# One core: recurrence and experts in halves of 512 rows, experts in whole fp32

## What is computed

```python
# recurrence, x after a layer norm; q, k rotated
q_r = einsum('bthd,hrd->bthr', q, Wq); k_r = einsum('bthd,hrd->bthr', k, Wk)
g = sigmoid(x @ g_w.T + g_b)
def step(M, inp):
    M = M * decay + einsum('bhr,bhd->bhrd', g_t * k_t * scale, v_t)
    y = einsum('bhr,bhrd->bhd', q_t, M)
hres = x + (Y @ out_w.T + out_b); result = layernorm(hres) * ln_g + ln_b
# experts, xt after a layer norm
scores = softmax(xt @ gate_w.T); top two: weights, idx
xs = xt * weight
for e in range(8):
    h = silu(xs @ w1[e].T + b1[e]); x2 = h @ w2[e].T + b2[e]; x3 = xs @ w3[e].T + b3[e]
    y += sum over the two choices of x2 * x3 * (idx == e)
z = silu(xt @ sw1.T) * (xt @ sw2.T) @ sw3.T
result = y + z
```

## Time and profile before

| | us |
|---|---|
| median of three runs | 2244.3 (2242.52 to 2247.84) |
| profiled execution | 2242.04, span 2240.0 |
| granted clock of TensorE, mean of the span | 0.978 |
| PE busy | 2057.9 (92%) |
| DVE busy | 1506.3 (67%) |
| ACT busy | 1309.4 (58%) |
| POOL busy | 1429.1 (64%) |

### The profile page before, as it was taken

How to read it: one execution, slowest core, us unless ns; L and a number is a source line. 1 busy time by engine, 2 the same in 40 slices (tenths; PEclk the granted TensorE clock), 3 DMA queues, 4 the chain that set the end, 5 groups by cost and what they waited for, 6 DMA issues and landing times. The chain is left out here.

```text
span 2240.0 us, 47860 instructions
## 1 busy us (share of the span) xinstructions
PE 2057.9 (92%) x19834; PEld 1531.2 (68%) x19834; DVE 1506.3 (67%) x1760; ACT 1309.4 (58%) x1585; POOL 1429.1 (64%) x652
## 2 busy tenths in 40 slices
PE   4799999999999999999999989999999777667998
PEld 3577777767777776777777767777777433215777
DVE  5666666766666667666666676666666247995685
ACT  2477767676767666677777676767676540002332
POOL 0277777777777777777777767777777622552464
PEclk8899999999999999999999999999999889997999
DMA  8010101111010112010001030101000030000320
GB/s 233 15 35 14 27 14 41 44 43 25 15 28 13 28 30 71 13 30 16 25 16 43 16 76 7 34 6 34 13 18 4 4 126 0 0 0 10 119 99 38
DMA packets 44669, 79.77 MB, mean 36 GB/s; under 512 B 7072, under 2 KB 31264, under 8 KB 43696
## 3 DMA queue, kind: packets, MB, share of 16 engines
q1 hardware_dynamic: 44464, 76.80, 12.2%
HBM read 70.03 MB, written 5.31 MB: 34 GB/s over the span
## 5 line engine op out<-in xcount | busy, mean ns | idle before, releaser
L764 POOL TENSOR_TENSOR acc<-acc,PR 128x1024 f32<-128x1024 f32 x480 | 1154.2, 2405 | 348.7 <-ACT PR L545 311.4
L620 DVE TENSOR_REDUCE amx<-ps 128x2 f32<-128x1024 f32 x512 | 626.9, 1224 | 387.4 <-PE ps L318 387.4
L545 ACT ACTIVATE PR<-ps 128x1024 f32<-128x1024 f32 x512 | 518.7, 1019 | 236.3 <-PE ps L326 236.3
L505 ACT ACTIVATE ps<-NM 128x1024 f32<-128x1024 f32 x416 | 427.2, 1028 | 189.3 <-DVE V L605 144.9
L334 PE MATMUL ps<-PR,V 128*64 128x256 f32 x4096 | 504.6, 389 | 0.1
L334 PEld LDWEIGHTS ps<-PR,V 128*64 128x64 f32 x4096 | 273.6, 138 | 163.3 <-issue 33.3
L326 PE MATMUL ps<-qh,KH 64*128 64x256 f32 x2048 | 329.2, 310 | 33.3 <-ACT ps L505 29.6
L300 PE MATMUL ps<-wv,C 64*128 64x256 f32 x4608 | 314.7, 280 | 0.0
L289 PE MATMUL ps<-C,wk 64*128 64x512 f32 x2304 | 311.2, 398 | 0.7 <-DVE x L654 0.7
L300 PEld LDWEIGHTS ps<-wv,C 64*128 64x128 f32 x4608 | 305.3, 186 | 8.4
L326 PE MATMUL ps<-ql,KH 64*128 64x256 f32 x2048 | 300.6, 280 | 0.0
(11 more groups left out here) (168 smaller groups left out, 1847.1 us busy)
## 6 DMA issues: line engine op xcount, KB each, us to landing
wk<-wk_split SPq DMA_DIRECT2D x62, 192.0 KB, 3.2
wv<-wv_split SPq DMA_DIRECT2D x30, 384.0 KB, 5.2
bc<-wm_rows SPq DMA_DIRECT2D x16, 512.0 KB, 5.0
craw<-in_ctx SPq DMA_DIRECT2D x30, 256.0 KB, 3.8
we<-in_we SPq DMA_DIRECT2D x8, 768.0 KB, 6.9
wo<-in_wo SPq DMA_DIRECT2D x68, 64.0 KB, 2.2
wq<-in_wq SPq DMA_DIRECT2D x32, 128.0 KB, 3.0
craw<-in_ctx SPq DMA_DIRECT2D x30, 128.0 KB, 4.0
```

Source lines behind the costliest of these rows:

```text
L505: act.activation(ps[:, first_bank:first_bank + 2, :].rearrange("p h (k n) -> p h k n", k=2), row.unsqueeze(2).to_broadcast([P, 2, 2, ROWS] ...
L545: act.activation(PR[:, pr_slot(t, hf), :, :, :].rearrange("p h k n -> p (h k n)"), ps[:, bank:bank + 2, :].rearrange("p h n -> p (h n)"), ...
L620: dve.tensor_reduce(amx[:, :, t, c], psG, AX.X, ALU.max).then_inc(g_max, 1)
L764: pool.tensor_tensor(flat(acc[:, :, :, :]), flat(acc[:, :, :, :]), flat(PR[:, pr_slot(t, hf), :, :, :]), ALU.add).then_inc(acc_done, 1)
```

## The change

`recurrence` and `experts` become one function, `tail`, in one block. Rows are taken in two halves of 512. The steps are now 64, of 512 rows each: half 0 group 0, half 0 group 1, then half 1 (J is the step, J // 16 its quarter). The norm, routing, shared expert and experts of half 0 are written into the order of the steps of half 1: three of them stand between the layers of each of the experts 0 to 3. The experts pass twice over the eight weights, in "expert turns" X of 0 to 15, the second time in reverse order (expert 7 first), so that weights that are still there need not be loaded again. A turn has the layers third(X), first(X + 1), second(X), each of two blocks into two banks, in turn 4, 5 and 6, 7.

Operands of the experts and of the shared expert's first layers are not split: a block is two fp32 matmuls on the numbers as they are. The splits on ACT, DVE and POOL are gone. The recurrence's values are split as before.

The order of the 16 columns in a quarter changes: the sum over ranks is made once for four steps, as four matmuls to four groups of 32 output partitions. POOL has four slots for its products. The shared output is computed after each half's shared products and added to the rows then. The shape of the output and what is computed stay.

The core of the diff (eight leading spaces are cut):

```diff
+def tail(nc, nb, top, d, out):
...
+raw_slot = {X: X % 3 for X in range(E)} | {8: 1, 9: 0, 10: 2, 14: 1, 15: 0}
...
+OPS = [(1, 0)] + [op for X in range(NX) for op in ((3, X), (1, X + 1), (2, X)) if op[1] < NX]
+op_index = {op: k for k, op in enumerate(OPS)}
...
+    load_expert(11, wl_in[0])
+    load_expert(12, wl_in[1])
+    for X in range(E):
+        if X == 6:
+
+            sp.wait_ge(x_done, NR)
+            load_expert(13, wl_in[2])
+            store_routes(1)
+        sp.wait_ge(t3m_ready, 2 * X + 2)
+        load_weights_of_rows(X + 2)
+        if X + 3 < E:
+            sp.wait_ge(x2_ps, 2 * X + 2)
+            load_expert(X + 3, we_in[X % 3])
...
-    def split_product(out, stationary, moving):
-
-        passes = [(a, b, t) for a, b in ((0, 0), (1, 0), (0, 1)) for t in range(2)]
-        for i, (a, b, t) in enumerate(passes):
-            mm = pe.matmul(out, stationary(a, t), moving(b, t), start=(i == 0), stop=(i == len(passes) - 1))
+            mm = pe.matmul(ps[:, bank, :], w4[:, i, t, g * P:g * P + P], uT[:, hf, t, :], start=(t == 0), stop=(t == 1))
...
+    def step(J):
+        n, s = J // STEPS, J % STEPS
+        g, dd = n % 2, 4 * (s % 4) + s // 4
+        if s == 0:
+            pe.wait_ge(vlo, n + 1)
+        if J >= 2:
+            pe.wait_ge(kv_ready, J - 1)
+        pe.matmul(ps[:, J % 2, :], selvr[:, dd, :], vh[:, g, :], start=True, stop=False)
+        pe.matmul(ps[:, J % 2, :], selvr[:, dd, :], vl[:, g, :], start=False, stop=True).then_inc(vb_ps, 1)
+        if J >= 6 and J % 4 == 2:
+            sum_r(J // 4 - 1)
+
+    def sum_r(q):
+
+        n, e = q // 4, q % 4
+        pe.wait_ge(qm_ready, 4 * q + 4)
+        if e == 0 and n:
+            pe.wait_ge(y_sb, n)
+        for k in range(4):
+            mm = pe.matmul(ps[32 * k:32 * k + 32, 2, :], sely[:, e, :], qm[:, k, :], start=(e == 0), stop=(e == 3), skip_group_check=True)
+        mm.then_inc(y_ps, 1)
...
+    def product(X, a, m, src, bank):
+        for t in range(2):
+            mm = pe.matmul(ps[:, bank, :], raw(X)[:, 2 * a + t, m * P:m * P + P], src[:, t, :], start=(t == 0), stop=(t == 1))
         return mm
...
+    def wait_bank(k, m):
+
+        if k >= 2:
+            layer, X = OPS[k - 2]
+            pe.wait_ge([t1_ready, xy_ready, t3_ready][layer - 1], 2 * X + m + 1)
...
+    def second_layer(X):
+        k = op_index[2, X]
+        pe.wait_ge(h_ready, 2 * X + 2)
+        for m in range(2):
+            wait_bank(k, m)
+            product(X, 1, m, hT[:, X % 2, :, :], op_bank(k, m)).then_inc(x2_ps, 1)
...
+    for n in range(3):
+        for s in range(STEPS):
+            step(STEPS * n + s)
+            if n == 1 and s == 0:
+                pe.wait_ge(na["t_sb"], 2 * HR)
+            if s == 0:
+                project_q(n + 1)
+            if s == 1:
+                project_k(n + 1)
...
+                    pe.wait_ge(ow_in, 32)
...
+                ranks(n + 1, s - 5)
+            if s == 7:
+                project_v(n + 1)
+            if n == 0 and s == 13:
+                pe.wait_ge(gate_ready, 2)
+                pe.wait_ge(vlo, 2)
+                transposes(na, 1, u, lambda r: 6 + r % HR // 2)
+            if n == 2 and s == 11:
+                pe.wait_ge(qr_ready, 4)
+                pe.wait_ge(kk_ready, 4)
+                transposes(nc4, 0, u, lambda r: wt_bank(0, r))
+            if n == 2 and s == 12:
+                pe.wait_ge(g_in, 32)
+                logits(0)
+                pe.wait_ge(sw_in, 16)
+                pe.wait_ge(gate_ready, 4)
+                pe.wait_ge(vlo, 4)
+                shared(0, 0)
+            if n == 2 and s == 13:
+                shared(0, 1)
+            if n == 2 and s == 15:
+                routes(0)
+    for s in range(4):
+        step(3 * STEPS + s)
+        if s in (0, 1):
+            shared(0, 2 + s)
     pe.wait_ge(s3_in, 16)
-    for r in range(NR):
-        if r >= 4:
-            pe.wait_ge(f_ready, r - 3)
-        for t in range(4):
-            pe.matmul(ps[:, r % 4, 0:DM], zT[:, t, r * P:r * P + P], sw3[:, t, :], start=(t == 0), stop=(t == 3))
-        for t in range(2):
-            mm = pe.transpose(ps[:, 4 + r % 4, t * P:t * P + P], yT[:, t, r * P:r * P + P], ident[:, :])
-        mm.then_inc(f_ps, 1)
+    shared_out(0, 0)
+    first_layer(0)
+    for X in range(4):
+        third_layer(X)
+        step(3 * STEPS + 4 + 3 * X)
+        if X == 0:
+            shared_out(0, 1)
+        first_layer(X + 1)
+        step(3 * STEPS + 5 + 3 * X)
+        second_layer(X)
+        step(3 * STEPS + 6 + 3 * X)
+    third_layer(4)
+    sum_r(15)
+    first_layer(5)
+    project_out(1, 0)
+    project_out(1, 1)
+    second_layer(4)
+    third_layer(5)
+    first_layer(6)
+    second_layer(5)
+    transposes(nc4, 1, u, lambda r: wt_bank(1, r))
+    third_layer(6)
+    logits(1)
+    shared(1, 0)
+    first_layer(7)
+    shared(1, 1)
+    second_layer(6)
+    shared(1, 2)
+    routes(1)
+    third_layer(7)
+    shared(1, 3)
+    first_layer(8)
+    second_layer(7)
+    shared_out(1, 0)
+    shared_out(1, 1)
+    for X in range(E, NX):
+        third_layer(X)
+        if X + 1 < NX:
+            first_layer(X + 1)
+        second_layer(X)
+        if X == E:
+            rows_of_y(0, 0)
+            rows_of_y(0, 1)
+    for i in range(2):
+        rows_of_y(1, i)
...
+    values_hi(2)
+    gates(3)
+    copy_y(1)
+    queries(3)
+    root(nbb, 0, st_b[2])
+    values_hi(3)
+    root(nc4, 0, st_c[2])
+    columns(nc4, 0, lambda r: wt_bank(0, r), wT[0])
+    exponentials(0)
+    act.wait_ge(be_in, 16)
+    for m in range(3):
+        shared_silu(0, m)
+    copy_routes(0)
+    shared_silu(0, 3)
+    copy_y(2)
+    for X in range(5):
+        hidden(X)
+    copy_y(3)
+    hidden(5)
+    root(nbb, 1, st_b[2])
+    hidden(6)
+    root(nc4, 1, st_c[2])
+    columns(nc4, 1, lambda r: wt_bank(1, r), wT[1])
+    exponentials(1)
+    shared_silu(1, 0)
+    shared_silu(1, 1)
+    hidden(7)
+    shared_silu(1, 2)
+    copy_routes(1)
...
+    def step(J):
+        n, s = J // STEPS, J % STEPS
+        g = n % 2
+        if s == 0:
+            dve.wait_ge(kk_ready, n + 1)
+        if J >= 2:
+            dve.wait_ge(m_done, J - 1)
+        dve.wait_ge(vb_ps, J + 1)
+        dve.tensor_tensor(kv[:, J % 2, :], ps[:, J % 2, :], kk[:, g, :], ALU.mult).then_inc(kv_ready, 1)
+        dve.wait_ge(kv_ready, J + 1)
+        if J >= 2:
+            dve.wait_ge(qm_ready, J - 1)
+        dve.tensor_tensor_scan(M[:, J % 2, :], dect[:, g, :], kv[:, J % 2, :], 0.0, ALU.mult, ALU.add).then_inc(m_done, 1)
...
+    for n in range(3):
+        for s in range(STEPS):
+            step(STEPS * n + s)
+            if s in (2, 3):
+                rotate(n + 1, s - 2)
+            if s == 7:
+                keys(n + 1)
+            if s == 8:
+                values_lo(n + 1)
+            if n == 0 and s == 9:
+                norm_stats(na, 1, row, st_a)
+            if n == 0 and s == 11:
+                norm_apply(na, 1, row, st_a)
+            if n == 2 and s in (4, 5):
+                add_out(0, s - 4)
+            if n == 2 and s == 5:
+                dve.wait_ge(h_added, 2)
+                norm_stats(nbb, 0, lambda r: u[:, r, :], st_b)
+            if n == 2 and s == 6:
+                scale_rows(0)
+            if n == 2 and s == 7:
+                add_rows(0)
+            if n == 2 and s == 8:
+                dve.wait_ge(x_done, HR)
+                norm_stats(nc4, 0, row, st_c)
+            if n == 2 and s == 9:
+                norm_apply(nc4, 0, row, st_c)
+            if n == 2 and s == 13:
+                dve.wait_ge(g_in, 32)
+                below_max(0)
+            if n == 2 and s == 14:
+                best_two(0)
+            if n == 2 and s == 15:
+                shared_product(0, 0)
+                shared_product(0, 1)
+    dve.wait_ge(be_in, 16)
+    for s in range(4):
+        step(3 * STEPS + s)
+        if s in (1, 2):
+            shared_product(0, s + 1)
+    add_shared(0, 0)
+    weigh_first(0)
+    for X in range(4):
+        weigh_third(X)
+        step(3 * STEPS + 4 + 3 * X)
+        if X == 0:
+            add_shared(0, 1)
+        mask_third(X)
+        step(3 * STEPS + 5 + 3 * X)
+        weigh_first(X + 1)
+        step(3 * STEPS + 6 + 3 * X)
+        second_by_third(X)
+    weigh_third(4)
+    mask_third(4)
+    weigh_first(5)
+    add_out(1, 0)
+    add_out(1, 1)
+    dve.wait_ge(h_added, 4)
+    norm_stats(nbb, 1, lambda r: u[:, r, :], st_b)
+    second_by_third(4)
+    scale_rows(1)
+    weigh_third(5)
+    add_rows(1)
+    mask_third(5)
+    dve.wait_ge(x_done, 2 * HR)
+    norm_stats(nc4, 1, row, st_c)
+    weigh_first(6)
+    second_by_third(5)
+    norm_apply(nc4, 1, row, st_c)
+    weigh_third(6)
+    mask_third(6)
+    below_max(1)
+    weigh_first(7)
+    shared_product(1, 0)
+    best_two(1)
+    second_by_third(6)
+    shared_product(1, 1)
+    weigh_third(7)
+    mask_third(7)
+    shared_product(1, 2)
+    shared_product(1, 3)
```

(40 more changed lines are left out.)

915 lines of the change are left out of this document (426 added, 489 removed).

## The result

The changed kernel takes 2249.41 us (median of 8 runs, 2247.67 to 2253.75), beside 2241.97 for the kernel before in the same rounds (2240.68 to 2247.84). The ratio is 1.0028, with a 95% interval of 1.0017 to 1.0039: slightly slower, and 31.9 us above the forecast of 2217.5. A second measurement, in the last experiment, gave 1.0021 (1.0011 to 1.0032). The profiled execution took 2251.76 us for a span of 2249.9.

A forecast was written before the change was run, and what follows sets the result against it. No one engine bounds the stages, which follow with little overlap; halves should overlap them. Five stages reach 2210.2, 3 us of clock gives span 2213.2, execution 2215.2, and 2.3 to the median gives 2217.5 us; range 2204 to 2240.

The forecast's parts named there:

- rival B: Rank sums on PE: column groups run one after another, 16 sums of 3.43 us, time 2241; chance 0.07.
- Rival A: Recurrence steps: DVE and POOL collide less than 64 times 0.6 us, 10 us less, 2207; chance 0.15.
- Stage 1: Up to the first step: one of four pairs projected first, first DVE product at 1836.6 instead of 1868.7.
- Stage 2: Steps until the product of step 9 of the third group: 42.4, 40.8 and 31.1 us, ending at 1950.9.
- Stage 3: From there to the third layer of expert 4: PE longer with 85.5 us, total 95 with waits, end 2045.9.
- about 0.5 us of slack: POOL's four product slots wait for the sum of the four before, which PE issues two steps later: about 0.5 us slack.
- The clock: PE's granted clock in projections and ranks: 3 us added, half of +6 for a fifth of 31 us at half speed.
- Stage 4: The rest after the third layer of expert 4: PE alone, 151.8 us, 4.0 wait, 1 for small waits, to 2202.7.
- Stage 5: The end: last DVE product, POOL's sum, transposes, two sums 4.4 us, then 3.1 to the span's end at 2210.2.
- C: Slower side: PE granted 1.2 GHz from group 0 until stage 3's layers, price 35 us, time 2252; chance 0.08.
- D: PE and DVE wait for each other in stages 3 and 4 more than read: +12 us, 2229; chance 0.15.
- E: A wait in the fixed orders ties the halves, so the change does not overlap: 2250 and more; chance 0.03.

The follow-up runs named there:

- the last experiment: The changed kernel, unedited, measured once more: 2248.0 us, ratio 1.0021 to the kernel before.
- e4: Changed kernel with eight slots instead of four for POOL's products, so a product waits for the rank sum of eight steps before: 2224.8 us.
- e5: Changed kernel with three edits: eight POOL slots, output pair 0 added a step earlier, biases(1) moved off the steps: 2219.8 us, ratio 0.9897 to the kernel before.
- e3: Changed kernel with POOL's biases(1) moved from between the products of steps 20 and 21 to after the sum of expert 3: 2244.4 us.
- e2: Changed kernel with the first half's output pair 0 added on DVE after step 3 of the third group instead of step 4: 2245.2 us.
- b_whole: Kernel before with the experts' products on whole fp32, splits still made but unused, next expert's weights loaded later: 2268.7 us, ratio 1.0108.
- e11: e5 with each expert product made of six matmuls on rounded numbers in a fixed tile, the layers' numbers left out: 2197.6 us.
- e7: e5 plus the first half's routing moved behind shared products, with broadcasts of steps 35 to 46 computed five times over: 2221.0 us.
- e9: e5 plus the first half's routing moved behind shared products, with broadcasts of steps 35 to 42 computed five times over: 2216.9 us.
- e8: Changed kernel with eight POOL slots, but the long reach used only in steps 8 to 47: 2235.3 us.

## Why the prediction was wrong

**Prices.** All held, the rank sum least well (13% over). A plain step is 2.43 to 2.44 apart, the scan alone 1.23 and beside POOL 1.81 (I had 1.24 and 1.75), POOL's product 1.27 (1.26), a whole product 1.72 (1.71), the four matmuls of a rank sum 1.07 (0.95):

```profile
1898.51 1.07 PE L1044 MATMUL ps<-qm,sely 128*32 128x512 f32 x8
```

That settles rival B: one after another they would be 3.43. By the Trainium skill, TensorE: Matmul & The Clock Gate, section Measured speedup vs the span model, three groups gave 2.38 times; four gave 3.2 times here (3.43 / 1.07), and the estimate of 1.1 us that I made by it was the closer of my two. Rival A (fewer collisions) has no trace: plain steps collide as computed. (Its own sum was off: a third of 64 x 0.6 and the 0.6 are 13.4 less, not 10.)

**Stage 1.** First product at 1839.45 in this profile for 1836.6: +2.8, within the scatter that this place has between kernels.

**Stage 2** took 130.4 us from the start of the first product to the end of that of step 41, for 114.3. **Stage 3** took 113.5 for 95. These two are the miss, and its steps are:
- "about 0.5 us of slack" for POOL's four slots. It is the step that failed most. I compared sum and product in a plain step, where it is nearly so, and carried it to the steps beside shared pairs and layers, where the broadcasts come 4 to 7 us apart and the sum, two products of POOL and the scan stand in one line. Measured by e4's columns without 41-45 and 51-52: 16.5 us, and with the 2.8 of clock in 51-52 that hang on the same wait, 19.3.
- POOL's biases(1), moved among the steps, was not in the sum at all: 4.1 us (e5 against e4, 16-32; 4.4 alone in e3).
- The projection of pair 1 behind DVE's sum of pair 0: I had read the bank that they share, but priced only the sum. 2.6 us (e5 against e4, 32-41); alone, in e2, 0.9. How the rest comes about is open.
- The clock: I added 3 us. The columns 41-45 and 51-52 cost 3.9 and 2.8 at 1.2 GHz, and the third shared pair 2.0 in 45-51 (5.59 for 3.6), which is in e5 too for the most part. The 3.9 differ from one execution to the next.

With 0.7 in 45-51, that of the third shared pair (4.89 in e5), the sum is 16.5 + 4.1 + 2.6 + 6.7 + 0.7 = 30.6, the difference of 245.0 and 214.4. That e5 comes within 0.6 us of the forecast in stage 3 is part luck: in 13 of the 15 profiles with these columns 41-45 has 1.9 to 4.6 us more. In e5, from which the three waits are gone, stage 3 takes 95.6 us by the scans (12.4 + 23.7 + 11.4 + 49.8 - 1.7, the third layer of expert 4 beginning 1.7 before scan 63, as in the changed kernel), for the 95 forecast, and stage 2 takes 117.8 (42.7 + 40.2 + 34.2 and one product), 3.5 over the forecast. The waits that I did count, 4.6 for the routing instructions and 4.0 ahead of the second half's transposes, are 4.79 and 4.92 in e5. (In the changed kernel the first is 7.43.)

**Stage 4** took 159.9 for 156.8, +3.1. Of that, 0.9 is the wait ahead of the transposes (4.92 for 4.0) and 1.4 the expert layer behind them, at 4.96 for the 3.60 of the other layers; the rest I didn't pursue.

```profile
2117.31 4.96 PE L1095 MATMUL ps<-wT,we 128*128 128x512 f32 x8
```

**Stage 5** took 6.6 for 7.5. No wait of SP's moved loads reached PE or DVE. The profile's own spans add +36.7 over the forecast's 2213.2, the medians 31.9; the rest is that this profile lay 2.3 above its median and the one before 2.3 under its own.

**The rivals.** C, the slower side, was right that PE falls to 1.2 GHz (0.78 to 0.87 in three stages) and wrong on what decides: not the steps with a projection (e5 took 42.7 and 40.2 in its first two groups, for the 42.4 and 40.8 forecast at full clock, with granted clocks of 0.84 and 0.79), but the few long PE works that DVE waits for, logits, shared pairs and first shared output, some 7 to 9 us. Its 2252, which counts the 3 us of clock twice (35 over 2214.5 is 2249.5), is near the measured time by luck. D named the coupling of PE and DVE beside the experts, with 12 us, but not POOL as the one in the middle. E asked for a wait in the orders that ties the halves, and it is the nearest in kind; I had given it 0.03 since I had read no such wait. It was on my list of moved waits, with its price too low. So not an unknown resource but a known wait made the error, and the chance of 0.82 for faster left no room for one.

**The balance of the change.** Whole fp32 in the experts costs 25 us in the kernel before (b_whole) and 22 at the other end (e11) by the medians, 30 and 26 by the stretches where the experts are. From b_whole to the changed kernel it is 19 less: the rest of the change (halves, overlap, rank sums in fours, no splits) pays for most of it. With the waits gone it brings 49 (2268.7 to 2219.8), and the whole change is then 1.0% faster than before.

## What to carry to other kernels

A buffer whose slots are freed by another engine is priced at the place where that engine issues the freeing work, in the longest of its surroundings: a slack that holds in a plain loop is gone once long work stands between the loop's steps. Where a step is interleaved by hand, list for each engine the furthest instruction it waits for and give each such wait a row of its own in the sum, the small ones on idle engines too. And when four waits of a few us each lie in one overlap, a forecast that assumes them all hidden should carry their sum as a rival with a real chance.

## What the runs showed of the hardware

Four groups of 32 columns run nearly side by side: the eight instructions of a rank sum, 512 rows each, took 1.07 us, where one after another, at 0.43, they would take 3.43. A scan with both inputs in SBUF took 1.23 us with POOL idle, 1.81 beside a POOL product of 1.27, 2.20 beside the second of two, and 3.29 when it was issued 0.14 after a POOL operation of 2.36 had begun. In the last three of these cases it ended 1.1 us after the end of the POOL operation that was under way when it was issued (1904.40 for 1903.33 in the last), though there another POOL operation followed at once. Repeated matmuls held the granted clock at 1.00 for 40 us (e7), and it fell again at PE's next waits, for the norm (1.00, then 0.86 in e9). The same program can meet either clock at the same instruction: the logits took 3.55 us in e4 and 2.01 in e8.
